# New orders for the tasks of all five engines in a four-layer graph network on one core

## The chip, the core and the metric

The kernel runs on one core of a Trainium2 chip. Five engines work side by side, each through its own list of instructions in order: TensorE (PE) multiplies, ScalarE (ACT) and VectorE (DVE) work elementwise, GpSimd (POOL) does a small power function here and issues three kinds of DMA, SyncE (SP) issues all others. They meet by semaphores alone. The metric is the device time of one launch in microseconds, the median of several runs.

## The reference

Sixteen graphs of 1024 nodes with 128 features pass through four layers that share one adjacency matrix; each layer's result is added to its input and normalised. Cut to what matters:

```python
x = _layernorm(x + relu(softmax(leaky_relu(s_i + t_j) + mask) @ H))           # layer 0, one head
x = _layernorm(x + elu(per head: softmax(leaky_relu(e_i + e_j) on edges) @ h)) # layer 1, 8 heads of 16
x = _layernorm(x + relu(layernorm((adj == 1) @ x / degree @ W + x @ self_w.T + b)))  # layer 2
x = _layernorm(x + per head: softmax(Wh @ Wh.T / sqrt(32) on edges) @ Wh)     # layer 3, 4 heads of 32
```

x is [16, 1024, 128] in float32, adj [16, 1024, 1024] in int32 with some 3% ones.

## The kernel before

Four batches are under way at once. Period f works on batch n = f + 1 in layer 0 and the preparation of layer 1, on batch f in the main part of layer 1, on batch k = f - 1 in layers 2 and 3, and on m = f - 2 in the end of layer 3. The periods run from f = -1 to 17; those of f = 2 to 14 all follow the same table, and f = 15 to 17 share one stretch.

**The work of a period.** Layer 1 has 32 pairs of units (`unit1`, 8 heads of 4): ACT, or for five pairs of a period DVE (`layer1_ramps`), makes a ramp of the source row of the head (`s1row`, three buffers); DVE masks it with the adjacency (L1672); PE multiplies it in (L1020, two units); DVE adds up each finished head (`head1`, L1680). `layer1_sum_all` (`sum1`, eight tiles, L1001) is a second sum on PE. For layer 2, PE does `layer2_self` and eight `layer2_sum` (L1067, L1070), ACT copies the self term to `yb`, and DVE takes both in `layer2_out` (from L1747), followed by statistics, affine part and `layer2_norm` (the DVE rows of L1483 that write `x` from `yb`). Its result is turned on PE (`layer3_turn`, L862 into `kp`), copied by ACT (`xbT`), projected (`layer3_project`, L1086 and L1092), copied twice by ACT (`w` and `shared`), and one half of the second copy is mirrored to the other partitions by two DMAs on SP (`spread_far`, L752), called the mirror copy below. The shift comes from the row maxima (`layer3_turn_maxima`, L1097). Then 16 times `layer3_scores` (L1122 where PE puts the mask in, and L1129), two exponentials on ACT (L1376), for eight of them a masking on DVE (L1818), and `layer3_values` on PE (L1146). `layer3_finish` on DVE (L1837) leads to the residual transfer on POOL (L822). Layer 0 has `layer0_turn` (L893), `layer0_project` (L905), its maximum and spread (L916, L920), eight units (L1272 on ACT, L1578 on DVE, L945 on PE), `layer0_finish` and `layer0_norm` (L1483 into `x`).

**The adjacency's way.** POOL copies a batch's matrix to a DRAM buffer as bf16 (`load_adjacency`, L829, "adjacency copy"), once the batch before has been turned out of that buffer. SP turns it by a DMA transpose (L734). POOL then narrows it to 8 bits in one of three buffers (`narrow_adjacency`, L818).

**What sets the order.** Each engine has tables that are written out by hand, one for each kind of period: a number for each task. `schedule` walks through the numbers and calls what has that number. The numbers of two engines have nothing to do with each other; only the order on each engine counts. What an engine waits for stands in the task's own code. The wait of `spread_sources` for a free buffer is by count: head h may be loaded when head h - 3 has all its edges.

Of the kernel before, what the change touches and what calls it, by code (L numbers as in the profile page):

```python
# [76 lines left out]
def graph_stack(nc, x, adj, L0_gnn_W, L0_gnn_a, L1_gnn_W, L1_gnn_a, L2_gnn_rel_weights, L2_gnn_self_w,  # L77
# [12 lines left out]
    B_RING, P_RING, P0_RING, R_RING, S_RING = 6, 4, 3, 6, 3  # L90
# [36 lines left out]
    with ExitStack() as ctx:  # L127
# [103 lines left out]
        rest2 = yf  # L231
# [260 lines left out]
        def schedule(tables, step):  # L492
# [3 lines left out]
            for stage, periods in zip(STAGE, SECTIONS):  # L496
                for s in range(STEPS):
# [23 lines left out]
            (dict(maxima1=93, maxima3=43, project0=[18, 20, 26], project1=89, project2=102, project3=40, scores3=[48,
                 52, 56, 60, 67, 69, 71, 73, 84, 85, 88, 90, 96, 98, 101, 103], self2=1, shift3=45, sources1=91,
                 spread0=46, spread1=95, sum1=[21, 22, 25, 29, 30, 31, 32, 33], sum2=[2, 3, 4, 5, 6, 11, 12, 13],
                 top0=36, turn0=[0, 17], turn1=87, turn2=99, turn3=37, turn_back=-1, unit0=[74, 75, 76, 77, 78, 79,
                 80, 81], unit1=[7, 8, 9, 10, 14, 15, 16, 19, 23, 24, 27, 28, 34, 35, 38, 39, 41, 42, 44, 47, 49, 50,
                 51, 53, 57, 58, 59, 61, 63, 64, 65, 66], values3=[54, 55, 62, 68, 70, 72, 82, 83, 86, 92, 94, 97,
                 100, 104, 105, 106]),),
            (dict(maxima1=92, maxima3=43, project0=[28, 29, 34], project1=90, project2=102, project3=41, scores3=[49,
                 53, 56, 58, 65, 70, 75, 82, 84, 86, 89, 93, 96, 100, 103, 105], self2=0, shift3=47, sources1=94,
                 spread0=48, spread1=97, sum1=[19, 24, 25, 26, 35, 36, 37, 38], sum2=[1, 2, 3, 6, 9, 12, 16, 17],  # L530
                 top0=44, turn0=[10, 20], turn1=88, turn2=98, turn3=39, turn_back=32, unit0=[72, 73, 74, 77, 78, 79,
                 80, 81], unit1=[4, 5, 7, 8, 11, 13, 14, 15, 18, 21, 22, 23, 27, 30, 31, 33, 40, 42, 45, 46, 50, 51,
                 52, 55, 59, 60, 61, 62, 66, 67, 68, 69], values3=[54, 57, 63, 64, 71, 76, 83, 85, 87, 91, 95, 99,
                 101, 104, 106, 107]),),
            (dict(maxima1=-1, maxima3=42, project0=[-1, -1, -1], project1=-1, project2=73, project3=39, scores3=[45,
                 47, 53, 58, 61, 63, 65, 66, 69, 72, 76, 79, 83, 90, 92, 93], self2=0, shift3=44, sources1=-1,
                 spread0=-1, spread1=-1, sum1=[16, 19, 24, 25, 28, 31, 32, 34], sum2=[1, 2, 3, 4, 8, 10, 13, 15],
                 top0=-1, turn0=[-1, -1], turn1=-1, turn2=71, turn3=35, turn_back=18, unit0=[-1, -1, -1, -1, -1, -1,
                 -1, -1], unit1=[5, 6, 7, 9, 11, 12, 14, 17, 20, 21, 22, 23, 26, 27, 29, 30, 33, 36, 37, 38, 40, 41,
                 43, 46, 48, 50, 51, 52, 55, 56, 57, 59], values3=[49, 54, 60, 62, 64, 67, 68, 70, 74, 75, 84, 89, 91,  # L540
                 94, 95, 97]), dict(maxima1=-1, maxima3=100, project0=[-1, -1, -1], project1=-1, project2=-1,
                 project3=98, scores3=[102, 103, 104, 107, 109, 111, 113, 115, 117, 119, 121, 123, 125, 127, 129,
                 131], self2=77, shift3=101, sources1=-1, spread0=-1, spread1=-1, sum1=[-1, -1, -1, -1, -1, -1, -1,
                 -1], sum2=[78, 80, 81, 82, 85, 86, 87, 88], top0=-1, turn0=[-1, -1], turn1=-1, turn2=-1, turn3=96,
                 turn_back=99, unit0=[-1, -1, -1, -1, -1, -1, -1, -1], unit1=[-1, -1, -1, -1, -1, -1, -1, -1, -1, -1,
                 -1, -1, -1, -1, -1, -1, -1, -1, -1, -1, -1, -1, -1, -1, -1, -1, -1, -1, -1, -1, -1, -1],
                 values3=[105, 106, 108, 110, 112, 114, 116, 118, 120, 122, 124, 126, 128, 130, 132, 133]),
# [21 lines left out]
            (dict(cut1=[84, 87], cut1_second=[93, 94], elu=57, exp3=[32, 33, 36, 37, 40, 41, 45, 46, 49, 50, 53, 54,
                 55, 56, 59, 61, 65, 66, 68, 69, 71, 72, 74, 75, 77, 78, 81, 82, 85, 86, 90, 91], exps0=31, exps1=79,  # L570
                 first2=88, out3=[52, 67, 80, 96], prepare0=43, project0=[10, 13, 16], project1=73, project3=25,
                 ramps=[2, 3, -1, 4, 5, 6, -1, 7, 9, 11, 12, 14, 15, 18, 20, 21, 24, 26, 28, -1, 29, 30, -1, 34, 35,
                 -1, 38, 39, 42, 44], ramps_ahead=[89, 95], second2=92, self2=1, sources1=76, sum1=[17, 19, 22],
                 turn0=[0, 8], turn1=70, turn2=83, turn3=23, unit0=[47, 48, 51, 58, 60, 62, 63, 64], wide3=27),),
            (dict(cut1=[83, 85], cut1_second=[89, 90], elu=66, exp3=[31, 32, 34, 35, 38, 39, 41, 42, 46, 47, 53, 54,
                 58, 59, 62, 63, 64, 65, 68, 69, 71, 72, 74, 76, 77, 78, 82, 84, 87, 88, 91, 92], exps0=37, exps1=79,
                 first2=86, out3=[49, 67, 81, 95], prepare0=48, project0=[15, 17, 25], project1=73, project3=26,
                 ramps=[0, 1, -1, 2, 3, 4, -1, 5, 6, 9, 10, 11, 13, 14, 16, 18, 19, 22, 28, -1, 29, 30, -1, 33, 36,
                 -1, 40, 43, 44, 45], ramps_ahead=[94, 96], second2=93, self2=8, sources1=75, sum1=[20, 21, 23],
                 turn0=[7, 12], turn1=70, turn2=80, turn3=24, unit0=[50, 51, 52, 55, 56, 57, 60, 61], wide3=27),),  # L580
# [108 lines left out]
        def _(sp):  # L689
# [1273 lines left out]
```

How the kernel before makes its waits and increments, by code:

```python
            def load(dst, src, done):  # L690
                sp.dma_start(dst, src).then_inc(done, 16)
# [4 lines left out]
            def load_x(b):  # L696
                if x1_ready.any_before(b):
                    sp.wait_ge(x1_ready.sem, x1_ready.before(b))
                sp.dma_start(x0[:], rows(x, b)).then_inc(x_loaded.sem, 16)
# [1 line left out]
            def spread_sources(b, h):  # L701
                if h >= S_RING:
                    sp.wait_ge(edges_ready.sem, edges_ready.of(b, (h - S_RING + 1) * T // 2))
                elif edges_ready.any_before(b):
                    sp.wait_ge(edges_ready.sem, edges_ready.before(b))
                sp.dma_start(s1row[:, h % S_RING, :], s1_dram[h:h + 1].broadcast_to([P, N])) \
                    .then_inc(s1_loaded[h].sem, 16)
# [1 line left out]
            def store_row(b):  # L710
                sp.wait_ge(row0_ready.sem, row0_ready.of(b))
                if s0_loaded.any_before(b):
                    sp.wait_ge(s0_loaded.sem, s0_loaded.before(b))
                sp.dma_start(s0_dram.rearrange("a (t p) -> (a t) p", p=P), row0[:]).then_inc(s0_stored.sem, 16)
# [1 line left out]
            def spread_row(b):  # L717
                sp.wait_ge(s0_stored.sem, s0_stored.of(b))
                sp.dma_start(c0[:], s0_dram.broadcast_to([P, N])).then_inc(s0_loaded.sem, 16)
# [1 line left out]
            def store_sources(b):  # L721
                sp.wait_ge(s1_copied.sem, s1_copied.of(b))
                if edges_ready.any_before(b):
                    for h in range(H1):
                        sp.wait_ge(s1_loaded[h].sem, s1_loaded[h].before(b))
```

## Time and profile before

| | us |
|---|---|
| median of 3 runs | 2438.4 |
| lowest, highest | 2432.07, 2440.47 |
| the profiled execution | 2435.11 |
| its span, first to last instruction | 2433.3 |

The profiled execution spends 1.8 us outside the span. Times of rows are counted from the span's start. A row of a timeline gives start, length, engine, line, operation, what it writes and reads, how often, and in square brackets how long its engine stood still before it and what it waited for. The mean granted clock of PE was 0.978 of full speed; it was below full in the first 180 us, in the last 100, and in three short dips between.

### The profile page before, as it was taken

What the parts mean: (1) busy time and instruction counts of PE and PEld (TensorE: products, weight loads), DVE (VectorE), ACT (ScalarE), POOL (GpSimd) and SP (SyncE); (2) the same over time, 40 slices, a digit from 0 to 9 for tenths busy, and PEclk for the clock granted to TensorE, in tenths of its full rate; (3) what the DMA queues carried; (4) which work ended last, traced back from release to release, by engine and by line L of the source; (5) the groups of instructions that cost most, each with busy time, mean ns of one, the idle gap of its engine ahead of it and who ended that gap; (6) DMA issues with size and microseconds to landing.
All of it is one profiled execution on the core that took longest, in us unless ns stands there. A gap on an engine that the chain in (4) does not pass through costs nothing.

```text
span 2433.3 us, 56856 instructions
## 1 busy us (share of the span) xinstructions
PE 2226.6 (92%) x23701; PEld 1498.8 (62%) x23701; DVE 1986.4 (82%) x4206; ACT 1946.5 (80%) x2166; POOL 180.4 (7%) x134
## 2 busy tenths in 40 slices
PE   6668999999999999999999999999999999998876
PEld 5667576575856657585665757566585765658431
DVE  4677788889888888988889888888988878897666
ACT  3958698887889878788987879898787988878734
POOL 0000000010000001000000100001010000100010
PEclk8879999999999999999999999999999999999989
DMA  4552061523315253341524324143432415301000
GB/s 92 140 114 71 5 145 53 121 75 92 82 47 132 59 113 80 76 92 45 131 71 105 88 54 114 44 123 79 105 89 45 114 53 123 80 27 48 24 18 18
DMA packets 190865, 193.77 MB, mean 80 GB/s; under 512 B 129368, under 2 KB 165328, under 8 KB 187728
## 3 DMA queue, kind: packets, MB, share of 16 engines
q1 hardware_dynamic: 183008, 132.99, 20.0%
q0 software_dynamic: 7600, 57.15, 12.0%
q8 instruction: 187, 3.06, 0.5%
q14 instruction: 70, 0.57, 0.1%
HBM read 151.26 MB, written 40.43 MB: 79 GB/s over the span
## 4 chain that ended last, share of the span: by engine, by line
PE 68%; ACT 11%; issue 6%; DVE 6%; DMA 2%; POOL 0%; SPq 0%; POOLq 0%; ACTq 0%; DVEq 0%
PE kp L1146 12%; PE fp L1020 10%; PE kp L1129 9%; PE fp L945 8%; PE kp L1001 7%; ACT weight L1376 5%; PE kp L1122 4%; PE kp L1070 4%; DMA shared<-shared 2%; PE kp L1067 2%; ACT ramp L1328 1%; PE fp L1038 1%; PE fp L869 1%; PE kp L1086 1%; PE kp L1163 1%
## 5 line engine op out<-in xcount | busy, mean ns | idle before, releaser
L1328 ACT ACTIVATE ramp<-s1row,tbig 128x1024 fp8e4<-128x1024 f32 x854 | 909.3, 1148 | 11.9 <-DVE weight L1672 11.9
L1376 ACT ACTIVATE weight<-kp,shift 128x1024 f32<-128x1024 f32 x480 | 511.2, 1111 | 206.4 <-PE kp L1129 188.3
L1146 PE MATMUL kp<-weight,w 128*33 128x512 f32 x1920 | 456.8, 599 | 17.9 <-DVE weight L1818 6.6
L1672 DVE TENSOR_TENSOR weight<-ramp,AT 128x512 int32<-128x512 int32 x512 | 343.3, 689 | 153.7 <-PE fp L1020 98.7
L1020 PEld LDWEIGHTS fp<-vh_parts,weight 128*128 128x128 fp8e4 x8192 | 389.9, 97 | 83.7 <-DVE weight L1672 41.2
L1020 PE MATMUL fp<-vh_parts,weight 128*128 128x102 bf16 x8192 | 417.6, 208 | 21.0 <-DVE weight L1672 15.5
L1818 DVE SCALAR_TENSOR_TENSOR weight<-AT,weight 128x1024 f32<-128x1024 fp8e4 x272 | 321.5, 1219 | 37.6 <-ACT weight L1376 37.3
L1129 PE MATMUL kp<-shared 32*128 32x512 f32 x1920 | 274.7, 641 | 13.8 <-ACT weight L1376 13.7
L1146 PEld LDWEIGHTS kp<-weight,w 128*33 128x33 f32 x1920 | 94.4, 110 | 312.7 <-issue 224.0
L945 PEld LDWEIGHTS fp<-features,weight 128*128 128x128 f32 x1840 | 207.9, 192 | 28.7 <-issue 27.0
L945 PE MATMUL fp<-features,weight 128*128 128x129 f32 x1840 | 213.4, 276 | 5.0 <-DVE weight L1578 4.9
L1001 PE MATMUL kp<-vh_parts,AT 128*128 128x136 bf16 x3072 | 212.5, 229 | 0.3 <-ACT vh_rest L1233 0.3
L1001 PEld LDWEIGHTS kp<-vh_parts,AT 128*128 128x128 fp8e4 x3072 | 205.0, 97 | 0.9 <-ACT vh_rest L1233 0.5
L1272 ACT ACTIVATE weight<-xfT,v0neg,v0s 128x1024 f32<-128x1024 f32 x123 | 149.4, 1244 | 37.2 <-PE fp L945 36.2
L1070 PE MATMUL kp<-elu,AT 128*128 128x128 bf16 x1920 | 171.8, 221 | 0.0
L1067 PE MATMUL kp<-y_hi,AT 128*128 128x129 bf16 x960 | 167.7, 222 | 2.7 <-DVE elu L1732 2.7
L1578 DVE SCALAR_TENSOR_TENSOR weight<-weight,v,AT 128x1024 f32<-128x1024 f32 x123 | 153.1, 1281 | 15.5 <-ACT weight L1272 14.8
L1680 DVE TENSOR_REDUCE vh<-fp 128x272 f32<-128x816 f32 x128 | 128.4, 1003 | 42.2 <-PE fp L1020 41.9
L1122 PE MATMUL kp<-AT,big 128*128 128x512 fp8e4 x480 | 127.6, 382 | 28.7 <-DMA shared<-shared 21.8
L1129 PEld LDWEIGHTS kp<-shared 32*128 32x128 f32 x1920 | 76.1, 183 | 125.7 <-issue 67.9
L1070 PEld LDWEIGHTS kp<-elu,AT 128*128 128x128 fp8e4 x1920 | 149.7, 98 | 0.2
L795 POOL TENSOR_TENSOR bsmall<-bsmall,half_neg 128x8 f32<-128x8 f32 x32 | 60.7, 1897 | 917.4 <-DVE bsmall L1478 917.4
(251 smaller groups left out, 2715.9 us busy)
## 6 DMA issues: line engine op xcount, KB each, us to landing
s1row<-s_rows_dram SPq DMA_DIRECT2D x128, 512.0 KB, 4.1
adj_bf_dram<-in_adj_dram POOLq DMA_DIRECT2D x15, 2048.0 KB, 13.3
AT<-turned POOLq DMA_DIRECT2D x15, 1024.0 KB, 7.5
x<-in_x_dram SPq DMA_DIRECT2D x16, 512.0 KB, 4.4
out_dram<-elu SPq DMA_DIRECT2D x16, 512.0 KB, 3.2
xfT<-s_row_dram SPq DMA_DIRECT2D x15, 512.0 KB, 4.6
shared<-shared SPq DMA_DIRECT2D x30, 256.0 KB, 3.5
elu<-x POOLq DMA_DIRECT2D x15, 512.0 KB, 4.7
```

Of the source, the lines that this page charges most:

```text
L945: last = pe.matmul(sums0(b)[:, g, n * (D + 1):(n + 1) * (D + 1)], ring0(b, jt)[:, t * P:(t + 1) * P], h0[:, jt, :], start=(jt == 0 and n = ...
L1001: last = pe.matmul(kp[:, SUM_A_BANKS[t // PER], n * H1 * C1:(n + 1) * H1 * C1].rearrange("p (h c) -> p h c", h=H1), AT[:, third, jt, t * P ...
L1020: last = pe.matmul(fp[:, 1 + t // 4, col:col + 2 * PARTS * C1], edges[:, u % B_RING, t * P:(t + 1) * P], vh_parts[:, jt, h, :, :, :].rearr ...
L1067: pe.matmul(sums2(b)[:, g, col:col + D + 1], lhsT, y2_hi[:, jt, :], start=(jt == 0), stop=False, skip_group_check=True)
L1070: last = pe.matmul(sums2(b)[:, g, col:col + D], lhsT, low2(b)[:, jt, k, :], start=False, stop=(jt == T - 1 and k == 1), skip_group_check=True)
L1122: pe.matmul(score_banks(b, w)[:, x, :], big[:], AT[:, third, 2 * J + x, n * HALF:(n + 1) * HALF], start=True, stop=False, skip_group_check ...
L1129: last = pe.matmul(score_banks(b, w)[:, x, :], mine[:, jt * P:(jt + 1) * P], mine[:, n * HALF:(n + 1) * HALF], start=v in masks(b), stop=True,
L1146: last = pe.matmul(kp[side(h), 0, :], values3(b)[:, (2 * J + x) * H3 + h, :], weight3[:, w % P_RING, x * HALF:(x + 1) * HALF], start=(J == ...
L1328: act.activation(ramp[:, u % R_RING, :], s1row[:, h % S_RING, :] if b or h else kp_pair, ACT.Relu, bias=tbig1[:, jt, h:h + 1], scale=BIG, ...
L1376: act.activation(weight3[:, w % P_RING, :], score_banks(b, w).rearrange("p a n -> p (a n)"), ACT.Exp, bias=shifts3(b)[:, h:h + 1], scale=R ...
L1672: dve.tensor_tensor(edge_words[:, u % B_RING:u % B_RING + 2, :], ramp_words[:, u % R_RING:u % R_RING + 2, :], AT_words[:, third, jt:jt + 2 ...
L1818: dve.scalar_tensor_tensor(out=mine, in0=AT[:, third, 2 * J:2 * J + 2, n * HALF:(n + 1) * HALF], scalar=0.0, in1=mine, op0=ALU.is_equal if ...
```

## The change

All numbers of the tables for PE, ACT, DVE, POOL and SP are new; no task is added or taken away. One wait is added, on SP, which concerns batch 0 alone. The diff of the tables is long and tells little, so one row of POOL's and SP's each stands for it:

```diff
@@ ON_POOL, periods f = 2 to 14
-            (dict(adjacency=6, narrow=1, residual3=3, rstd0=5, rstd1=7, rstd2=0, rstd3=2, rstd_tail=4),),
+            (dict(adjacency=3, narrow=4, residual3=2, rstd0=6, rstd1=7, rstd2=0, rstd3=1, rstd_tail=5),),
@@ ON_SP, periods f = 2 to 14
-            (dict(adjacency=0, far=5, out=10, sources=[2, 3, 4, 7, 9], sources_ahead=[12, 13, 14], spread_row=8,
-                 store_row=6, store_sources=11, x=1),),
+            (dict(adjacency=0, far=7, out=10, sources=[3, 2, 5, 4, 6], sources_ahead=[13, 14, 12], spread_row=9,
+                 store_row=8, store_sources=11, x=1),),
@@ spread_sources
                     sp.wait_ge(edges_ready.sem, edges_ready.before(b))
+                if b == 0 and h == S_RING:
+                    sp.wait_ge(s1_loaded[0].sem, s1_loaded[0].of(0))
                 sp.dma_start(s1row[:, h % S_RING, :], s1_dram[h:h + 1].broadcast_to([P, N])) \
```

The numbers of `sources` are those of heads 3, 4, 5, 6 and 7. So SP now issues head 4's row before head 3's, head 6's before head 5's, and head 7's before the mirror copy. Line numbers behind L706 are higher by 2 in the changed kernel.

POOL in one steady period, before: from the first of two layer-2 statistics (`bsmall`) to batch n's last statistic (`fsmall` is layer 1's).

```order
L795 TENSOR_TENSOR bsmall<-bsmall,half_neg 128x8
L818 DMA AT<-turned 128x8192
L795 TENSOR_TENSOR bsmall<-bsmall,half_neg 128x8
L822 DMA elu<-x 128x1024
L795 TENSOR_TENSOR tsmall<-tsmall,half_neg 128x8
L795 TENSOR_TENSOR small<-small,half_neg 128x8
L829 DMA adj_bf_dram<-in_adj_dram 64x16384
L795 TENSOR_TENSOR fsmall<-fsmall,half_neg 128x8
```

The same period of POOL, after:

```order
L797 TENSOR_TENSOR bsmall<-bsmall,half_neg 128x8 x2
L824 DMA elu<-x 128x1024
L831 DMA adj_bf_dram<-in_adj_dram 64x16384
L820 DMA AT<-turned 128x8192
L797 TENSOR_TENSOR tsmall<-tsmall,half_neg 128x8
L797 TENSOR_TENSOR small<-small,half_neg 128x8
L797 TENSOR_TENSOR fsmall<-fsmall,half_neg 128x8
```

The adjacency copy moved from behind layer 0's statistic (`small`) to right behind the residual transfer (`elu<-x`), and the narrowing transfer (`AT<-turned`) from ahead of that transfer to behind it.

PE in a steady period, before, from the last `layer1_sum_all` to the first scores:

```order
L1001 MATMUL kp<-vh_parts,AT 128x136 x96
L862 MATMUL kp<-ident,x 128x128 x8
L1020 MATMUL fp<-vh_parts,weight 128x102 x16
L1086 MATMUL kp<-rhs,xbT 128x128 x8
L1092 MATMUL kp<-xbT,rhs 128x512 x2
L1020 MATMUL fp<-vh_parts,weight 128x102 x16
L1097 MATMUL kp<-ident,qmax 4x128
L916 MATMUL fp<-ident,st 33x128
L1020 MATMUL fp<-vh_parts,weight 128x102 x32
L1101 MATMUL kp<-qdiag,ones 128x4
L920 MATMUL fp<-tmost,ones 128x1
L1122 MATMUL kp<-AT,big 128x512 x4
```

The same stretch of PE, after:

```order
L864 MATMUL kp<-ident,x 128x128 x8
L1022 MATMUL fp<-vh_parts,weight 128x102 x16
L907 MATMUL fp<-rhs,xfT 128x130 x2
L1088 MATMUL kp<-rhs,xbT 128x128 x8
L1094 MATMUL kp<-xbT,rhs 128x512 x2
L1022 MATMUL fp<-vh_parts,weight 128x102 x16
L1099 MATMUL kp<-ident,qmax 4x128
L1022 MATMUL fp<-vh_parts,weight 128x102 x16
L1103 MATMUL kp<-qdiag,ones 128x4
L1022 MATMUL fp<-vh_parts,weight 128x102 x16
L1124 MATMUL kp<-AT,big 128x512 x4
```

Layer 0's third projection (L907) came in ahead of `layer3_project`, and the maximum of layer 0 and its spread (L916 and L920 before) went behind the first scores. On ACT the copy of the self term now stands ahead of layer 0's first copy; in the period of f = 0, DVE does `layer0_finish` before the last four pairs of units and not behind them.

## Rows read from the trace of the kernel before

**Rows 1.** The page's first part: busy time, share of the span, instructions.

```profile
PE 2226.6 (92%) x23701; PEld 1498.8 (62%) x23701; DVE 1986.4 (82%) x4206; ACT 1946.5 (80%) x2166; POOL 180.4 (7%) x134
```

**Rows 2.** Windows view, one steady period: stretch, length, busy time by engine, PE clock, DMA.

```profile
1382.53:1525.84 143.31, 136.86 (x1479) 92.21 (x1479) 122.21 (x261) 121.27 (x136) 11.11 (x8) 1.00 0.36 86
```

**Rows 3.** Waits of PE in that period: total us, times, longest.

```profile
PE kp L1097 <- DVE qmax L1796: 1.4, 1, 1.4
PE kp L1122 <- DMA shared<-shared: 1.3, 1, 1.3
PE kp L1129 <- ACT weight L1376: 1.0, 2, 0.5
PE fp L1020 <- DVE weight L1672: 0.7, 1, 0.7
PE fp L905 <- ACT features L1233: 0.6, 1, 0.6
PE kp L1086 <- ACT xbT L1233: 0.4, 1, 0.4
```

**Rows 4.** Timeline of PE, from the end of layer 2's sums to the first scores.

```profile
1493.87 0.88 PE L1020 MATMUL fp<-vh_parts,weight 128*128 128x102 bf16 x16
...
1512.03 0.68 PE L905 MATMUL fp<-rhs,xfT 128*128 128x130 f32 x4
...
1518.83 1.04 PE L862 MATMUL kp<-ident,x 128*128 128x128 f32 x8
...
1520.98 2.05 PE L1086 MATMUL kp<-rhs,xbT 128*128 128x128 f32 x16 [0.40 <-ACT xbT L1233]
...
1530.35 1.02 PE L1122 MATMUL kp<-AT,big 128*128 128x512 fp8e4 x4 [1.31 <-DMA shared<-shared]
```

**Rows 5.** Timeline of DVE: the start of `layer2_out` and `layer2_norm`.

```profile
1494.30 0.29 DVE L1747 TENSOR_SCALAR deg<-kp 128x3 f32<-128x3 f32 x3 [0.70 <-ACT yb L1233]
...
1515.33 2.14 DVE L1483 TENSOR_SCALAR x<-yb,bsmall 128x128 f32<-128x128 f32 x8
```

**Rows 6.** Timeline of POOL: its three DMA issues of a period.

```profile
1442.32 0.58 POOL L829 DMA_DIRECT2D adj_bf_dram<-in_adj_dram  x1
...
1503.03 0.59 POOL L818 DMA_DIRECT2D AT<-turned  x1
...
1515.72 0.96 POOL L822 DMA_DIRECT2D elu<-x  x1 [0.46 <-DVE elu L1837]
```

**Rows 7.** The mirror copy: its issue on SP, and all its landings.

```profile
1525.84 1.11 SPq L752 DMA_DIRECT2D shared<-shared  x2
...
DMA to landing us min/median/max: 2.9/3.5/3.9
```

**Rows 8.** DMA view of 1442.32 to 1456, the adjacency copy: packets, MB, share; landing.

```profile
DMA packets 89, 2.15 MB, mean 157 GB/s; under 512 B 16, under 2 KB 16, under 8 KB 23
...
q0 software_dynamic: 80, 2.10, 75.8%
...
adj_bf_dram<-in_adj_dram POOLq DMA_DIRECT2D x1, 2048.0 KB, 13.6
```

**Rows 9.** DMA view of 83.92 to 85.30: a source row issued behind the narrowing transfer.

```profile
q0 software_dynamic: 33, 0.27, 98.1%
...
s1row<-s_rows_dram SPq DMA_DIRECT2D x1, 512.0 KB, 5.5
```

**Rows 10.** DMA view of 1498.91 to 1500.29: a source row alone.

```profile
q1 hardware_dynamic: 12, 0.05, 17.6%
...
s1row<-s_rows_dram SPq DMA_DIRECT2D x1, 512.0 KB, 3.7
```

**Rows 11.** Timelines of ACT and DVE at the end of the period f = 0.

```profile
149.52 1.02 ACT L1233 ACTIVATE xfT<-fp 128x1024 f32<-128x1024 f32 x1 [12.26 <-PE fp L862]
...
138.05 0.13 DVE L1589 RECIPROCAL rec<-kp 128x3 f32<-128x3 f32 x1
...
145.33 2.14 DVE L1483 TENSOR_SCALAR x<-x,small 128x128 f32<-128x128 f32 x8 [0.87 <-POOL small L795]
```

More of the change, by code:

```diff
@@ L521, in graph_stack @@
[L521 to L527, printed above, removed]
@@ L569, in graph_stack @@
[L569 to L574, printed above, removed]
@@ L575, in graph_stack @@
[L575 to L580, printed above, removed]
@@ new lines, in graph_stack @@
+            (dict(cut1=[82, 85], cut1_second=[93, 95], elu=62, exp3=[33, 34, 36, 37, 39, 40, 43, 44, 46, 47, 52, 55,
+                 59, 61, 63, 64, 65, 66, 68, 69, 71, 72, 74, 75, 78, 79, 83, 84, 87, 88, 90, 91], exps0=41, exps1=76,
+                 first2=86, out3=[54, 67, 80, 96], prepare0=48, project0=[9, 16, 27], project1=73, project3=28,
+                 ramps=[0, 1, -1, 2, 3, 6, -1, 8, 10, 11, 13, 14, 15, 17, 18, 21, 22, 23, 24, -1, 26, 30, -1, 31, 32,
+                 -1, 35, 38, 42, 45], ramps_ahead=[89, 94], second2=92, self2=4, sources1=77, sum1=[12, 19, 20],
+                 turn0=[5, 7], turn1=70, turn2=81, turn3=25, unit0=[49, 50, 51, 53, 56, 57, 58, 60], wide3=29),),
@@ new lines, in graph_stack @@
+            (dict(cut1=[83, 86], cut1_second=[89, 90], elu=64, exp3=[32, 33, 35, 36, 40, 41, 43, 44, 46, 47, 53, 54,
+                 58, 59, 62, 63, 65, 66, 68, 69, 71, 72, 74, 75, 77, 78, 82, 84, 87, 88, 91, 92], exps0=39, exps1=80,
+                 first2=85, out3=[49, 67, 81, 96], prepare0=48, project0=[18, 23, 29], project1=73, project3=26,
+                 ramps=[0, 1, -1, 2, 3, 4, -1, 5, 6, 8, 9, 10, 11, 12, 15, 16, 19, 21, 25, -1, 28, 30, -1, 31, 34, -1,
+                 37, 38, 42, 45], ramps_ahead=[94, 95], second2=93, self2=7, sources1=76, sum1=[13, 20, 22],
+                 turn0=[14, 17], turn1=70, turn2=79, turn3=24, unit0=[50, 51, 52, 55, 56, 57, 60, 61], wide3=27),),
@@ L659, in graph_stack @@
         ON_POOL = [
[L660 to L666 removed]
+            (dict(adjacency=0, narrow=-1, residual3=-1, rstd0=1, rstd1=-1, rstd2=-1, rstd3=-1, rstd_tail=-1),),
@@ L667, in graph_stack @@
         ]
         ON_SP = [
-            (dict(adjacency=-1, far=-1, out=-1, sources=[-1, -1, -1, -1, -1], sources_ahead=[1, 2, 3], spread_row=-1,
+            (dict(adjacency=-1, far=-1, out=-1, sources=[-1, -1, -1, -1, -1], sources_ahead=[3, 1, 2], spread_row=-1,
                  store_row=-1, store_sources=0, x=-1),),
-            (dict(adjacency=1, far=-1, out=-1, sources=[2, 3, 4, 5, 8], sources_ahead=[10, 11, 12], spread_row=7,
-                 store_row=6, store_sources=9, x=0),),
-            (dict(adjacency=0, far=7, out=-1, sources=[1, 2, 3, 8, 9], sources_ahead=[11, 12, 13], spread_row=6,
-                 store_row=5, store_sources=10, x=0),),
@@ L675, in graph_stack @@
-            (dict(adjacency=0, far=5, out=10, sources=[2, 3, 4, 7, 9], sources_ahead=[12, 13, 14], spread_row=8,
-                 store_row=6, store_sources=11, x=1),),
-            (dict(adjacency=-1, far=4, out=6, sources=[0, 1, 2, 3, 5], sources_ahead=[-1, -1, -1], spread_row=-1,
+            (dict(adjacency=1, far=-1, out=-1, sources=[3, 2, 4, 8, 7], sources_ahead=[10, 12, 11], spread_row=6,
+                 store_row=5, store_sources=9, x=0),),
+            (dict(adjacency=1, far=7, out=-1, sources=[2, 4, 3, 6, 5], sources_ahead=[13, 12, 11], spread_row=9,
+                 store_row=8, store_sources=10, x=0),),
@@ L678, in graph_stack @@
+            (dict(adjacency=0, far=7, out=10, sources=[3, 2, 5, 4, 6], sources_ahead=[13, 14, 12], spread_row=9,
+                 store_row=8, store_sources=11, x=1),),
+            (dict(adjacency=-1, far=4, out=6, sources=[1, 0, 3, 2, 5], sources_ahead=[-1, -1, -1], spread_row=-1,
                  store_row=-1, store_sources=-1, x=-1), dict(adjacency=-1, far=7, out=8, sources=[-1, -1, -1, -1, -1],
```

180 lines of the change are left out of this document (93 added, 87 removed).

## The prediction

> **What bounds the kernel now.** I read the busy shares first: TensorE (PE) is busy 92% of the span, no other engine more than 82% [rows 1]. So only what lets PE stand still can be won or lost by an order. Then I cut out one period of the steady part, from one issue of the mirror copy to the next: 143.31 us with PE busy 136.86, so 6.45 us idle, at full granted clock [rows 2]. Thirteen periods (f = 2 to 14) run by this table and repeat it. The waits of PE in that period [rows 3] name the losses: 1.4 for the row maxima of layer 3, 1.3 for the mirror copy (the DMA inside `shared`), 1.0 for exponentials, 0.7 for edge weights, 0.6 and 0.4 for two ScalarE (ACT) copies. The profiled execution took 2435.1 us (span 2433.3); the median of the runs is 2438.4, so 3.3 is added at the end.
>
> **Part 1, the new order on PE, VectorE (DVE) and ACT in the 13 steady periods.** Nothing is added or removed, so durations stay and I follow starts. All times here are in the period shown.
> Three waits of PE stand between the end of layer 2's sums (1493.87) and `layer3_project` (1520.98): 0.74 before a unit of edges, 0.65 between two `layer0_project`, 0.40 before `layer3_project` [rows 3, 4]. In the new order two `layer1_sum_all` stand ahead of the first, three between the second pair, and a `layer0_project` covers the copy before the third: 1.8 us of waits lose their cause. What is late next is DVE. `layer2_out` starts at 1494.30, held by ACT's copy of the self term, and DVE then works without a pause to 1517.37 = 1515.33 + 2.04 (the eight tiles of `layer2_norm`, until the next start): 23.07 us [rows 5]. PE begins `layer3_turn` at 1518.83 [rows 4], 1.46 behind it. ACT's copy moves ahead of a copy of about 0.5, so DVE starts some 0.45 earlier and ends at 1516.9. PE: 24.96 us from 1493.87 to 1518.83, less 0.74 and 0.65, less 0.5 (the third `layer0_project`, a row at 1512.03 [rows 4], goes behind) plus 0.4 (a `layer0_turn` that comes in), is 23.5; begun at 1493.4, as that turn left the part before, it arrives at 1516.9 too. So `layer3_turn` starts near 1517.0, with the copies of ACT queued behind each other `layer3_project` near 1519.4, 1.6 earlier than 1520.98. From there to the first scores 9.4 us pass (1520.98 to 1530.35 [rows 4]), through two copies, the mirror copy and its landing; PE only waits in them, so the two tiny tasks that the new order takes out of this stretch (`layer0` maximum and its spread, 0.2) save nothing here.
> Behind the first scores PE had no wait for 29 us. There ACT gets the exponents of layer 0 between two pairs of exponentials, and three edge ramps stand before others; following PE, ACT and DVE task by task I find one new wait of 0.2. Later the scores of pair 11 move ahead of `layer1_turn_maxima` and `layer1_sources`, which takes away the 0.44 in the 1.0 of exponentials. Sum: 1.6 - 0.2 + 0.4 = 1.8; since I neglect semaphore latencies I take 1.6 per period, from 0.3 (DVE or ACT late at `layer3_turn`) to 1.9. 13 x 1.6 = 20.8 us gained.
>
> **Part 2, the new order of the DMA issues.** This is where I expect the loss. POOL issued the adjacency copy (2 MB) at 1442.32, when no other transfer was under way, and the narrowing transfer at 1503.03, both far from the mirror copy at 1525.84 [rows 6, 7]. Now both stand behind the residual transfer, which waits for `layer3_finish` and goes at 1515.72 [rows 6]; with DVE 0.5 earlier and `layer3_finish` ahead of one unit that is near 1514.8, and the adjacency copy follows at once, near 1515.8. It needs 13.6 us to land; its 64 large packets (80 less 16 under 512 B) kept 16 engines busy for 75.8% of 13.68 us, so 4 packets of 2.6 us on each engine [rows 8]. Behind the residual's own 3 us they would fill 1519 to 1529. On SP the last source row (head 7) now stands ahead of the mirror copy; it is issued near 1521.3 and its 8 packets per engine come first. The mirror copy is issued near 1524.2, in the middle of all that, and must land before PE may go on: its 2.9 to 3.9 us [rows 7] have no slack, as PE already waits 1.3 for it.
> What such a meeting costs: a source row issued at 83.92, while the narrowing transfer was under way, got no packet in its first 1.38 us (all 33 were the other's, 98.1% of the engines) and landed after 5.5 us [rows 9]; an undisturbed one had 12 packets in the same 1.38 us and landed after 3.7 [rows 10]. That is +1.8 us against packets of 0.66 us (98.1% of 16 x 1.38 us over 33), though the overlap was short. The engines thus do not share finely; a transfer waits for its turn. Bounds for the mirror copy: 1.2 (bandwidth shared in halves during its 1.2 us of data) and, for turns of one large packet ahead of each of its two halves, 2 x 2.6 = 5.2 in the slowest engine. I take 3.0, between one turn (half a packet, 1.3, plus the source row's 0.7) and two (3.9). 12 periods load a further adjacency (f = 2 to 13): 12 x 3.0 = 36 us lost; from 14 to 62.
> The Trainium skill (DMA: Bandwidth & Descriptors, Queues, rings and completion order) says that an engine changes between rings only at packet boundaries, and that a semaphore's write waits for every earlier write of that engine, whatever its queue. By that rule alone both turns are paid, 5.2 us, and the sum below would be 26 us higher. The trace agrees with the turns [rows 9], the second half of the rule no row shows.
>
> **Part 3, the first batches.** ACT waits 12.26 us at the end of the period f = 0 for batch 1's layer 0: DVE does `layer0_finish` from 138.05 to 143.46 (145.33 less a wait of 0.87 for POOL and the 1.00 of a head) and only then `layer0_norm` [rows 11]. It now stands ahead of the last four units, in time in which ACT was the slow one: 5.4 + 0.9 = 6.3 gained. Against it the adjacency copy of batch 2 moves from behind this point to right behind the narrowing transfer that [rows 9] shows under way, where the source rows of heads 4 and 3 are loaded; by [rows 9] 1.8 for one, and I take 2.3. Net -4, from -8 to +2. **The added wait**: SP waits, once, for head 0's row of batch 0, ahead of head 3's; that row is issued with the first three, and head 3's can go only when head 1's edges are made, which the whole of ACT's ramps for two heads precede. Behind it queue head 3's row and batch 1's layer 0 row. Nobody waits: 0. The tables of the last periods differ in single neighbours: 0, within 2.
>
> **Sum.** 2435.1 - 20.8 + 36 - 4 = 2446.3, plus 3.3: **2450 us**, 0.5% slower. Its own range, with 2.0 to 4.5 for the mirror copy: 2438 to 2468.
>
> **The rivals.**
> A, not slower: the mirror copy gets through (the engines' turns are short or the adjacency copy begins later than I place it), while part 1 holds. 2435.1 - 20.8 - 4 + 3.3 = 2414. For it: the slack elsewhere is real, and [rows 9] shows small packets against small ones only. Against it: no slack at the mirror copy. It decides from 1.6 us downwards: below that the periods get shorter. 20%.
> B, about equal: delay 1.2 to 2.0, 2428 to 2438, most of it within 0.3%. 20%.
> C, much slower: an engine finishes all it has of POOL's transfers before the mirror copy: 1529 plus up to 5.4 us of narrowing (8 packets of 0.66) against 1525.3, so 4 to 9 us; with 8, 2435.1 - 24.8 + 96 + 3.3 = 2510. [Rows 9] is what such a run-out looks like. 10%.
> D, part 1 fails: `layer3_norm`'s input comes late and a wait at `layer3_turn` replaces the three removed; gain 0.3 a period, delay 3.0: 2435.1 - 4 - 4 + 36 + 3.3 = 2466. 10%.
> Forecast: 40%.
>
> **How the numbers follow.** A measurement of this kernel tells 0.3%, 7.3 us, from no change. Faster by more (below 2431): A and a third of B, 27%. Within: the rest of B and the low end of the forecast, 18%. Slower: 55%. The range 2412 to 2472 leaves out C and little else.
>
> **What would show it.** Right: PE's wait for the mirror copy grows from 1.3 to 3 or more per period, the landing of that DMA from 3.5 to 6 or so, in 12 periods, the residual at once followed by the adjacency copy; PE's waits for `features`, `xbT` and edge weights gone; ACT's 12.3 halved. The steady period would be 144.7. Wrong: a period of 141.7 with the mirror copy at 3.5 (A), or a wait of PE at `layer3_turn` over 0.5 (D). If the adjacency copy were issued before 1510 in this frame, part 2 falls altogether.

## The result and the profile after

| | before | after |
|---|---|---|
| median, us | 2437.3 (4 runs) | 2570.3 (4 runs) |
| lowest, highest | 2432.07, 2440.47 | 2569.34, 2571.48 |
| the profiled execution's span | 2433.3 | 2567.6 |

The ratio is 1.055, interval 1.053 to 1.056: 5.5% slower. I had forecast 2450 and a range up to 2472; the direction was right and the size was not, nor did the range hold it.

The page of the changed kernel, its first part (busy time and share), against [rows 1]; TensorE does the same 23701 instructions, is busy 34.5 us longer and yet has a smaller share of the span.

```profile
PE 2261.1 (88%) x23701; PEld 1521.8 (59%) x23701; DVE 1985.5 (77%) x4206; ACT 1943.1 (76%) x2166; POOL 186.4 (7%) x134
```

One steady period, from one mirror copy to the next, as in [rows 2] (stretch, length, busy time of PE, of its weight loads, DVE, ACT and POOL, granted clock, DMA share, GB/s), and PE's waits in it, against [rows 3].

```profile
1459.89:1614.95 155.06, 139.57 (x1479) 93.57 (x1479) 122.07 (x261) 121.10 (x136) 11.54 (x8) 0.96 0.33 77
```

```profile
PE kp L1124 <- DMA shared<-shared: 12.2, 1, 12.2
PE kp L1099 <- DVE qmax L1798: 1.4, 1, 1.4
PE kp L864 <- DVE x L1485: 0.5, 1, 0.5
PE kp L1131 <- ACT weight L1378: 0.5, 1, 0.5
```

The period is 11.75 us longer than the 143.31 of [rows 2]. PE stands still for 155.06 - 139.57 = 15.49 us against 6.45. Of this the wait for the mirror copy went from 1.31 to 12.20 (+10.89), and all other waits together from 5.14 to 3.29 (-1.85). The remaining 2.71 is busy time: the same 1479 matmuls took 139.57 and not 136.86, at a granted clock of 0.96 and not 1.00.

Over the whole launch, by the issues of the mirror copy (line 752 before, 754 after; starts and length on SP): the first rows of after are

```profile
233.42 1.17 SPq L754 DMA_DIRECT2D shared<-shared  x2
372.33 1.11 SPq L754 DMA_DIRECT2D shared<-shared  x2
...
2236.42 1.89 SPq L754 DMA_DIRECT2D shared<-shared  x2
```

and the second and the fourteenth issue of before were at 377.47 and 2100.65. So after is 5.1 us ahead at the second mirror copy; then come twelve periods of 155.34 on average (1864.09 / 12) against 143.60 (1723.18 / 12), 140.9 lost; behind them the rest of the launch is 1.5 shorter (331.2 against 332.7). -5.1 + 140.9 - 1.5 = 134.3, the difference of the spans. It is all in the twelve periods in which POOL issues a further adjacency copy.

The timeline of POOL in the changed kernel, the place of [rows 6]: all three transfers now go within 2 us, 10 us ahead of the mirror copy at 1459.89.

```profile
1449.67 0.93 POOL L824 DMA_DIRECT2D elu<-x  x1 [0.49 <-DVE elu L1839]
1450.30 0.85 POOL L831 DMA_DIRECT2D adj_bf_dram<-in_adj_dram  x1
1450.84 0.87 POOL L820 DMA_DIRECT2D AT<-turned  x1
```

Landings of the mirror copy in the changed kernel, against 2.9/3.5/3.9 in [rows 7], and PE at the first scores, against [rows 4]:

```profile
DMA to landing us min/median/max: 3.1/14.7/16.1
```

```profile
1475.40 1.86 PE L1124 MATMUL kp<-AT,big 128*128 128x512 fp8e4 x4 [12.20 <-DMA shared<-shared]
```

Two DMA views of the changed kernel say what the engines did meanwhile. From the issue of head 7's source row (1456.64, just ahead of the mirror copy on SP) not one packet of SP's queue q1 was served for 3.5 us; all belonged to POOL's queue q0, in packets of 32 KB:

```profile
q0 software_dynamic: 30, 0.98, 130.5%
```

Then, from 1462.9 to 1470, the two queues were served strictly in turn, one packet of the one and one of the other:

```profile
q0 software_dynamic: 113, 0.84, 58.8%
q1 hardware_dynamic: 114, 0.45, 17.6%
```

An engine gave 0.59 us on average to each packet of POOL's and 0.17 to each of SP's (58.8% and 17.6% of 16 x 7.1 us, over the counts). That is the suspicion the experiments test: **each packet of the mirror copy pays one whole packet of POOL's, and so does each packet of the source row that stands ahead of it in the same queue, as long as POOL's queue has any.** A row of 512 KB is 8 packets of 4 KB for each engine, a half of the mirror copy 4; the under-512-byte packets in these views are extra ones, which I take for the semaphores' writes and count as one turn for each transfer: 9 + 5 + 5 = 19 turns.

POOL's queue had fewer left. Of the adjacency copy it was the last of four packets on each engine, of the narrowing transfer (128 packets of 8 KB) eight. From 1460.15 to 1465 the engines served 18 packets of q0 and 18 of q1, from 1465 to 1471 135 and 136; then q0 ran out. This is the view of the rest, 1471 to 1475.4, in which 0.48 MB of the mirror copy's 0.52 are served:

```profile
q1 hardware_dynamic: 150, 0.48, 40.3%
q0 software_dynamic: 25, 0.07, 8.2%
```

So the source row ahead of it paid nearly all of the turns, and the mirror copy came behind the row and behind nearly everything that POOL had issued. 19 turns of 0.59 + 0.17 us would be 14.4, from 1460.15 to 1474.6, and PE's wait ended at 1475.40; that this comes near is luck, as only some nine turns were that dear, the one beside a 32 KB packet much dearer, and the last ten cheaper.

### The profile page after: what moved, and what is told of

The parts are those of the page before. It is cut to its first block, busy times and chain, and to the rows that moved or that the text cites. A ratio compares the mean times of both kernels' runs of the same rounds, so it can differ in the third digit from the quotient of the medians.

```text
span 2567.6 us, 56857 instructions
## 1 busy us (share of the span) xinstructions
PE 2261.1 (88%) x23701; PEld 1521.8 (59%) x23701; DVE 1985.5 (77%) x4206; ACT 1943.1 (76%) x2166; POOL 186.4 (7%) x134
## 4 chain that ended last, share of the span: by engine, by line
PE 58%; ACT 15%; DMA 9%; DVE 9%; issue 8%; SPq 0%; POOL 0%; ACTq 0%; POOLq 0%; DVEq 0%
PE kp L1148 14%; PE kp L1131 11%; ACT ramp L1330 10%; PE fp L947 8%; DMA shared<-shared 8%; PE fp L1022 7%; PE kp L1124 5%; ACT weight L1378 2%; PE kp L1003 2%; PE fp L871 2%; PE kp L1072 1%; PE fp L864 1%; PE fp L1040 1%; PE kp L1088 1%; DVE weight L1674 1%
## 5 line engine op out<-in xcount | busy, mean ns | idle before, releaser
L1022 PE MATMUL fp<-vh_parts,weight 128*128 128x102 bf16 x8192 | 434.8, 211 | 20.5 <-DVE weight L1674 15.1
L1022 PEld LDWEIGHTS fp<-vh_parts,weight 128*128 128x128 fp8e4 x8192 | 401.8, 99 | 80.3 <-DVE weight L1674 41.5
L1131 PE MATMUL kp<-shared 32*128 32x512 f32 x1920 | 284.4, 663 | 10.3 <-ACT weight L1378 10.1
L1124 PE MATMUL kp<-AT,big 128*128 128x512 fp8e4 x480 | 138.8, 406 | 156.8 <-DMA shared<-shared 153.8
L947 PEld LDWEIGHTS fp<-features,weight 128*128 128x128 f32 x1840 | 210.8, 193 | 34.3 <-issue 32.7
L947 PE MATMUL fp<-features,weight 128*128 128x129 f32 x1840 | 219.0, 279 | 0.7 <-DVE weight L1580 0.7
L1124 PEld LDWEIGHTS kp<-AT,big 128*128 128x128 bf16 x480 | 37.8, 100 | 227.4 <-issue 163.0
## 6 DMA issues: line engine op xcount, KB each, us to landing
shared<-shared SPq DMA_DIRECT2D x30, 256.0 KB, 14.7
```

What stands on the lines that cost most here:

```text
L947: last = pe.matmul(sums0(b)[:, g, n * (D + 1):(n + 1) * (D + 1)], ring0(b, jt)[:, t * P:(t + 1) * P], h0[:, jt, :], start=(jt == 0 and n = ...
L1022: last = pe.matmul(fp[:, 1 + t // 4, col:col + 2 * PARTS * C1], edges[:, u % B_RING, t * P:(t + 1) * P], vh_parts[:, jt, h, :, :, :].rearr ...
L1124: pe.matmul(score_banks(b, w)[:, x, :], big[:], AT[:, third, 2 * J + x, n * HALF:(n + 1) * HALF], start=True, stop=False, skip_group_check ...
L1131: last = pe.matmul(score_banks(b, w)[:, x, :], mine[:, jt * P:(jt + 1) * P], mine[:, n * HALF:(n + 1) * HALF], start=v in masks(b), stop=True,
```

## Experiments

Theory 1 is that the meeting of POOL's transfers with the mirror copy makes the whole loss. In its form 1a the engines change the queue after every packet; in form 1b they finish POOL's packets first. The two differ in time only where POOL's queue still has packets when the mirror copy is through; in the changed kernel, by the view above, it has none. Theory 2 is that the new orders of PE, ACT and DVE carry a good part.

| kernel | median us | ratio to before, interval | PE's wait for the mirror copy, us in all |
|---|---|---|---|
| e1: POOL's old table in the changed kernel | 2411.1 | 0.989, 0.988 to 0.991 | 12.4 |
| e2: POOL's new table in the kernel before | 2579.8 | 1.058, 1.056 to 1.060 | 135.0 |
| e3: changed, mirror copy ahead of head 7's row | 2550.7 | 1.046, 1.045 to 1.048 | 138.7 |
| e4: changed, narrowing back | 2506.8 | 1.029, 1.027 to 1.030 | 100.1 |
| e5: changed, adjacency copy back | 2445.9 | 1.003, 1.002 to 1.005 | 34.3 |
| e6: changed, adjacency copy in 8 KB packets | 2566.0 | 1.053, 1.050 to 1.055 | 151.4 |
| e7: the same in 2 KB packets | 2489.1 | 1.022, 1.020 to 1.023 | 72.3 |
| e8: before, mirror copy delayed | 2553.9 | 1.048, 1.047 to 1.050 | 95.1 |
| e9: e1 again | 2408.8 | 0.989, 0.988 to 0.990 | 13.7 |
| e10: e9, mirror copy ahead of head 7's row | 2413.4 | 0.991, 0.990 to 0.993 | 16.0 |

The kernel before waits 21.8 us for it in all, the changed one 153.8.

**e1, POOL's order back.**

```diff
-            (dict(adjacency=3, narrow=4, residual3=2, rstd0=6, rstd1=7, rstd2=0, rstd3=1, rstd_tail=5),),
+            (dict(adjacency=6, narrow=1, residual3=3, rstd0=5, rstd1=7, rstd2=0, rstd3=2, rstd_tail=4),),
```

and so for the tables of POOL in the other stages.

> The changed kernel with the old table of POOL alone; PE, ACT, DVE and SP keep the new one. Theory 1 (the loss is the meeting of POOL's two transfers with the mirror copy): the mirror copy lands again after 3.5 to 4 us, PE waits 1 to 2 us for it, the period is 141.5 to 142, the granted clock is back at 0.975 or more, and the time is some 2412 us, ratio 0.99 to before. Theory 2 (a good part of the loss comes from the new orders of PE, ACT and DVE, and the mirror copy only shows it): over 2445 us. If the source row that now stands ahead of the mirror copy matters by itself: 2 us more a period, 2436.

2411.1 us: theory 2 falls, and with it the idea that a source row ahead of the mirror copy costs anything while POOL is quiet. The whole table of POOL is worth 159 us, and what is left of the change is a gain of 1.1%. One of its periods at full clock, and one that is not:

```profile
1370.37:1511.87 141.50, 137.05 (x1479) 92.58 (x1479) 122.09 (x261) 120.98 (x136) 11.55 (x8) 1.00 0.36 87
...
1084.00:1227.89 143.89, 139.80 (x1479) 93.75 (x1479) 122.07 (x261) 121.20 (x136) 11.55 (x8) 0.98 0.36 85
```

141.50 is what the prediction gave for part 1 alone (141.7). But only two of twelve periods are so; they take 142.7 on average.

**e2, POOL's order alone.** The same table, the other way round: the new one in the kernel before, where the mirror copy stands ahead of head 7's row.

> The kernel before with the new table of POOL alone; on SP the mirror copy stands ahead of head 7's source row. Theory 1a (an engine changes between the queues after every packet, so that each of the mirror copy's 8 packets of an engine waits for one of POOL's): the landing takes 9 to 11 us, PE's wait grows by 6 to 7, with 1 more for the clock 12 x 7.8 = 94 us, 2530. Theory 1b (the engines finish all of POOL's packets first): landing 14 to 15 us as in the changed kernel, 2570 to 2590. My prediction's single turns: landing 6 to 7, 2475.

2579.8: of the numbers given beforehand, this fits that of 1b and not that of 1a. A period of e2 and PE's largest wait in it:

```profile
1472.06:1628.26 156.20, 140.19 (x1479) 94.01 (x1479) 122.55 (x261) 121.30 (x136) 10.63 (x8) 0.96 0.34 79
```

```profile
PE kp L1122 <- DMA shared<-shared: 10.9, 1, 10.9
```

The DMA views show the order. From the mirror copy's issue to 1476.9 only POOL's queue was served, with 32 KB packets (first fence); from 1477 to 1482 both queues, packet for packet (second), so POOL's packets had not gone first.

```profile
q0 software_dynamic: 17, 0.56, 78.6%
...
shared<-shared SPq DMA_DIRECT2D x2, 256.0 KB, 11.6
```

```profile
q0 software_dynamic: 111, 0.78, 74.5%
q1 hardware_dynamic: 114, 0.40, 21.2%
```

What my number for 1a lacked is first the entry, as I call the time from a transfer's issue to its first packet: 4.9 us, in which 17 large packets began, one on each engine behind the one under way. And it lacked the narrowing: ten turns (2 x 5) beside its eight packets on each engine, at 0.76 us, are 1477 + 7.6 = 1484.6; PE went on at 1486.14. With ten turns against eight packets both forms end at nearly the same time, so the total of e2 can't tell them apart.

**e3, mirror copy first.**

```diff
-            (dict(adjacency=0, far=7, out=10, sources=[3, 2, 5, 4, 6], sources_ahead=[13, 14, 12], spread_row=9,
+            (dict(adjacency=0, far=6, out=10, sources=[3, 2, 5, 4, 7], sources_ahead=[13, 14, 12], spread_row=9,
```

> The changed kernel with head 7's source row behind the mirror copy in the steady periods. Theory 1a (a turn for every packet, and the source row's 8 packets an engine stand in the same queue ahead of the mirror copy): landing 10 to 11 us and not 14.7, some 5 us less a period with the clock, 2510. Theory 1b (all of POOL's packets first): no change, 2570.

2550.7, 20 us less and not 60: a third of what 1a gave, and more than the nothing of 1b. In the DMA view of its mirror copy at 1451.66 the entry is long again. Up to 1457.4, 5.7 us, three packets of q1 in all were served (first fence); then 1:1 (second, 1457.5 to 1464).

```profile
q0 software_dynamic: 32, 1.05, 98.2%
q1 hardware_dynamic: 3, 0.01, 0.6%
```

```profile
q0 software_dynamic: 136, 1.01, 76.0%
q1 hardware_dynamic: 133, 0.48, 24.9%
```

In the changed kernel the source row, issued 3.3 us ahead, had made that entry for the mirror copy. With the row behind it, the mirror copy pays the entry itself, and its own ten turns still take it through nearly all of the narrowing's eight packets. The two halves land 12.7 us after the issue on average, against 14.3 in the changed kernel's period; 1.6 us a period is the 20 us.

**e4 and e5, one transfer at a time.** Of POOL's table in the steady periods, e4:

```diff
-            (dict(adjacency=3, narrow=4, residual3=2, rstd0=6, rstd1=7, rstd2=0, rstd3=1, rstd_tail=5),),
+            (dict(adjacency=4, narrow=1, residual3=3, rstd0=6, rstd1=7, rstd2=0, rstd3=2, rstd_tail=5),),
```

> The changed kernel with the narrowing transfer back between the two statistics of layer 2; the adjacency copy stays right behind the residual transfer. Theory 1a: the adjacency copy's last packets end some 12 us after the residual's issue, then the source row and the mirror copy run freely; landing 6.5 to 8 us, PE waits 4 to 5, 8 to 9 us less a period than in the changed kernel, 2465 to 2475. Were the adjacency copy alone the cause: 2560. Were the narrowing alone the cause: 2415.

and e5:

```diff
-            (dict(adjacency=3, narrow=4, residual3=2, rstd0=6, rstd1=7, rstd2=0, rstd3=1, rstd_tail=5),),
+            (dict(adjacency=6, narrow=3, residual3=2, rstd0=5, rstd1=7, rstd2=0, rstd3=1, rstd_tail=4),),
```

> The changed kernel with the adjacency copy back behind layer 0's statistic, some 70 us away from the mirror copy, and the narrowing transfer left behind the residual transfer. Theory 1a (a turn for every packet): the narrowing's 8 packets of 0.62 us an engine end before the mirror copy's first packet comes, the landing is 3.5 to 4.5 us, the time 2411 to 2422. Theory 1b (POOL's packets first) says the same here; if the narrowing alone were a cause as large as the 64 us by which e4 and the changed kernel differ: 2475.

2506.8 and 2445.9. Against e1, the adjacency copy alone costs 96 us, the narrowing alone 35, both 159. Both numbers were expected smaller (2470; 2411 to 2422), so neither transfer is harmless there, and both together cost 28 us more than the sum of the two. (e1 has POOL's old tables in the other stages as well, which e4 and e5 have not; there they are worth 4 us, 1.7 up to the second mirror copy and 2.4 from the fourteenth on.) In e4 the turns are to be seen at their dearest: from 1423 to 1427, with the source row and the mirror copy waiting, POOL's 32 KB packets and SP's 4 KB packets were served one for one,

```profile
q0 software_dynamic: 24, 0.79, 94.4%
q1 hardware_dynamic: 24, 0.10, 6.5%
```

2.5 us for each of POOL's (94.4% of 64 us over 24). In these 4 us the queue of small packets got 6.5% of the engines. In e5 the landing's median is 4.5 us where e1 has 3.5, and PE waits 34.3 in all, 22 more; of the other 13 of the 35 us, 10 are busy time of PE (2260.3 against 2249.9 us for the same matmuls).

**e6 and e7, the size of the packets.** The same bytes, in an order that cannot be joined to longer packets (g = 16, c = 4 for 8 KB; g = 64, c = 1 for 2 KB); this is e6:

```diff
-                pool.dma_start(adj_dram, adj[bass.ds(b, 1)].rearrange("b i j -> (b i) j")) \
+                pool.dma_start(adj_dram.rearrange("(a g c) j -> g a (c j)", g=16, c=4),
+                               adj[bass.ds(b, 1)].rearrange("b (a g c) j -> g (b a) (c j)", g=16, c=4)) \
```

> The changed kernel; the adjacency copy walks through the same 2 MB in an order that makes packets of 8 KB, not 32 KB. Theory 1a (a turn for every packet): the source row gets its first turn some 2 us earlier and the mirror copy follows earlier: landing 11 to 12 us, 3 to 4 us less a period with the clock, 2520 to 2530. Theory 1b (POOL's packets first, so that only the bytes count): no change, 2570.

> As e6, in packets of 2 KB. Theory 1a: a turn of the adjacency copy costs 0.16 us, the 16 packets of source row and mirror copy an engine pass at 0.33 us each, the mirror copy lands after some 5 us, PE waits 2.4 and the time is near 2426 to 2440, though nothing is moved away. Theory 1b: 2570.

2566.0 and 2489.1. With 2 KB the loss falls by 81 us though POOL and SP issue in the changed kernel's order and the same bytes are carried; under 1b next to nothing could have moved. 8 KB changed next to nothing, where I had expected 45 us. The views of e6 (1452.49 to 1455.8, then 1456 to 1468) show why:

```profile
q0 software_dynamic: 87, 0.71, 103.0%
```

```profile
q0 software_dynamic: 251, 1.93, 81.6%
q1 hardware_dynamic: 253, 0.91, 22.0%
```

The first 3.3 us again belong to POOL's queue alone, with packets of 8 KB as with packets of 32 KB: the entry does not shrink with the packet. And 251 to 253 is one for one at 0.62 and 0.17 us, 0.79 us a turn, which for 19 turns is 15.0 us, from 1455.9 to 1470.9; e6's mirror copy, issued at 1455.27, had its halves landed 13.2 us later on average, and PE's wait of 11.6 ended at 1470.81. POOL's queue had some 16 packets left on each engine, about as many as SP had turns: as in the changed kernel, the mirror copy got through only when nearly all of POOL's bytes had gone, and these bytes are the same in packets of 8 KB. That is why the time stayed. With 2 KB the packets of q0 cost 0.19 us each (62.6% of 16 x 8 us over 419, from 1409 to 1417), behind an entry of 3.3 us that is wholly POOL's (340 packets):

```profile
q0 software_dynamic: 340, 0.70, 111.3%
```

```profile
q0 software_dynamic: 419, 0.86, 62.6%
q1 hardware_dynamic: 294, 1.03, 40.9%
```

SP's cost 0.18 (40.9% over 294). 19 turns of 0.37 us are 7.0; the median landing is 7.6 us, against 14.7. My 5 us for it had left out the entry. Here SP's turns ran out first. When PE went on, at 1418.10, POOL's queue still had nearly the whole narrowing transfer (1.05 MB) to serve, as the view from there to 1424 shows; this is what tells 1a from 1b.

```profile
q0 software_dynamic: 154, 0.99, 80.9%
```

**e8, the price of standing still.** In the kernel before, ahead of each mirror copy:

```diff
                 sp.wait_ge(wT_ready.sem, wT_ready.of(b))
+                for i in range(4):
+                    sp.dma_start(pause_row[0:1, :], L2_gnn_ln_beta.rearrange("(a d) -> a d", a=1)).then_inc(paused.sem, 16)
+                    sp.wait_ge(paused.sem, paused.of(b, 16 * (i + 1)))
                 for side in range(2):
```

> The kernel before; ahead of each mirror copy SP makes four DMAs of 512 bytes, one after the other, and waits for each: PE stands some 8 us longer, with next to no traffic beside it. Theory K (standing still lowers the clock granted afterwards): PE's busy time in a period grows from 136.9 to 139 or more though it does the same work, and the period grows by 2 to 3 us more than the wait. If it was the DMA traffic that slowed PE in the changed kernel: busy time stays 136.9, the period grows by the wait alone. Time by K: 15 x 10.5 = 158 over before, 2595; without: 2555.

2553.9. The total equals the number given for the other theory, but by accident: the four small DMAs took 4.8 us, not 8 (their first was issued at 1445.06, the mirror copy at 1449.87). A period of e8, and PE's wait in it:

```profile
1449.87:1600.31 150.44, 139.15 (x1479) 93.03 (x1479) 122.62 (x262) 121.36 (x136) 10.67 (x8) 0.98 0.35 82
```

```profile
PE kp L1127 <- DMA shared<-shared: 6.1, 1, 6.1
```

7.13 us longer than [rows 2]: 4.84 of standing still and 2.29 of busy time, for the same work, at a clock of 0.98, with the same DMA traffic but for a few bytes. Theory K stands: the busy time that the changed kernel loses is the clock's, and not the traffic's.

**e9 and e10, the version that beats both.** e9 is e1's kernel; e10 has e3's edit in it as well.

> The kernel of e1 once more, beside the next one on the same chip: 2411 us, 1.1% under before, if e1 stands.

> e1's kernel with head 7's source row behind the mirror copy in the steady periods, as before. By the turns, the source row's packets are through when the mirror copy's come, since none of POOL's stand between: nothing gained, 2409 to 2413. If the row ahead in the queue delays the mirror copy by itself: PE's wait for it falls by 0.3 to 0.5 us a period, with the clock 2405 or less.

e1's gain repeats: 2408.8, 1.1% under the kernel before. e10 at 2413.4 (2405.0 to 2418.1) can't be told from it: head 7's row ahead of the mirror copy is harmless with POOL quiet.

## Why the prediction was wrong in size

**Part 1, the orders of PE, DVE and ACT: the waits right, the total in part luck.** 1.6 to 1.8 us a period were forecast. In the changed kernel the waits other than for the mirror copy fell by 1.85. The three waits named are gone; in their place stands 0.52 at `layer3_turn` for DVE's `layer2_norm`, close to the forecast that PE and DVE arrive there together. It is just over the 0.5 that was named as rival D's sign, but D's gain of only 0.3 a period is out: without POOL's part (e1) a period at full clock is 141.50, forecast 141.7. The launch of e1 took 2411, forecast 2414 as rival A, and there luck helped. Its twelve periods gave 10.4 us (1723.18 against 1712.82) where 12 x 1.6 = 19 were forecast, since ten of them were not at full clock. The first batches (6.8) and the end of the launch (3.8) made up for it.

**Part 2, the DMA issues: the place right, the size wrong by 3.6.** Everything was late where the text put it: the transfers' order, no slack at the mirror copy, the source row's packets first. Forecast were 3.0 us a period from bounds of 1.2 and 5.2; measured 10.89. The step that failed is "turns of one large packet ahead of each of its two halves": it let the mirror copy pay once for each half. An engine changes the queue behind each packet (114 to 113 in the view above), so every packet in SP's queue pays, and those ahead of the mirror copy pay first. In its place the runs showed a mirror copy that came behind nearly all that POOL had issued, with PE's wait 10.89 us longer. Three terms were left out:
- the source row's packets, for which I took their own duration (0.7), pay turns too: the row stood against the last 32 KB packet and nearly the whole narrowing, to 1471;
- the narrowing transfer, behind the adjacency copy, is part of what has to go first (from 1465 to 1471, 0.62 us a packet); I had let it count in rival C alone;
- the entry: 3.3 to 3.5 us pass before a source row's first packet, and up to 5.7 before the mirror copy's (e3). What makes it was not tested.

The row on which I rested, [rows 9], was read amiss, and so was the agreement with turns for which the prediction cites it. 33 packets to none in 1.38 us looked like a transfer that holds the engines for a turn. But an undisturbed transfer has no packet either in its first 0.89 us (1498.91 to 1499.80, the one of [rows 10]), so this was mostly the entry, and hardly a turn is in it. Its +1.8 us was a price with little of the other queue left behind it, not one for a meeting of full length. Rival C had the nearest number (8 us, 2510) and 10% of the chance. Its mechanism, that the engines finish POOL's packets first, is not what e7 and the views of e2 and e3 show. Its outcome, that the mirror copy waits for all of POOL's transfers with the narrowing among them, is what the changed kernel did.

**The clock: left out.** The sum counted waits and took durations as fixed. A longer wait of PE is followed by matmuls at the lower clock. Windows of the changed kernel around the wait that ended at 1475.40 (the clock is the third number from the end):

```profile
1459.89:1463.20 3.31, 2.19 (x35) 1.86 (x35) 2.81 (x9) 3.31 (x6) 0.00 (x0) 1.00 1.18 210
1463.20:1469.00 5.80, 0.00 (x1) 0.00 (x0) 2.94 (x4) 3.21 (x4) 0.00 (x0) 0.84 0.67 167
1469.00:1475.40 6.40, 0.00 (x0) 0.03 (x1) 0.00 (x0) 0.00 (x0) 0.00 (x0) 0.50 0.67 165
1475.40:1480.00 4.60, 4.60 (x20) 1.64 (x21) 0.29 (x2) 0.62 (x1) 0.00 (x0) 0.50 0.01 4
1480.00:1485.00 5.00, 5.00 (x72) 3.60 (x70) 3.46 (x6) 3.69 (x4) 0.00 (x0) 0.92 0.34 106
```

While PE stood, the clock went from 2.4 to 1.2 GHz (1.00 to 0.50), and it stayed there through the first 4.6 us of full work. It costs 2.7 us in this period; over the twelve periods PE is busy 1674.5 us and was 1645.4 before, 29 us of the 134.

**Part 3, the first batches: the number right by luck.** Forecast -4; after is 5.1 ahead at the second mirror copy. ACT's wait of 12.26 became 4.94:

```profile
157.06 1.02 ACT L1235 ACTIVATE xfT<-fp 128x1024 f32<-128x1024 f32 x1 [4.94 <-PE fp L864]
```

But the row starts 7.5 us later than the 149.52 of [rows 11], and at the first mirror copy after is 7.2 behind (233.42 against 226.16). The term that was too small is the adjacency copy brought forward, taken at 2.3: e1, which leaves it late, has its first mirror copy at 225.20, 8.2 earlier than after. What it held up was not the source rows of heads 4 and 3 alone but also layer 0's row, which goes through DRAM behind them in SP's queue. Both kernels issue its store at 96.86; SP issued the reload at 100.64 in e1 and at 111.81 in after, and DVE waited:

```profile
DVE xfT L1562 <- DMA xfT<-s_row_dram: 7.8, 1, 7.8
```

The way from 7.2 behind to 5.1 ahead lies between the first two mirror copies (138.91 us, before 151.31) and was not taken apart. The added wait of SP was put at nothing; e1 holds it as well and is 6.8 ahead at the second mirror copy, so no loss of its shows. The tables of the last periods: -1.5, forecast 0 within 2.

Put together, with the one period shown for all twelve: 12 x (10.89 - 1.85 + 2.71) = 141.0, less 5.1 and 1.5, is 134.4, of which the forecast had 36 - 20.8 - 4 = 11.

## What to carry to other kernels

A small transfer on which the busiest engine waits must be priced, when it meets bulk transfers of another queue, by **turns**. Take the entry (here 3.3 to 5.7 us). Then count on each engine its packets and all packets ahead of it in its own queue, and beside it what the bulk queue still has. Each turn costs one packet of both queues, until one queue is empty; where the bulk queue is empty first, as here, the small transfer has waited for all of it. So keep bulk issues away from such a place by their own length. Where they can't be moved, cut them so small that the turns run out before the bulk does: 2 KB for 32 KB gave back 81 of the 134 us here, 8 KB next to nothing. Add to a new wait of TensorE the clock that it costs afterwards. And before the gain of a new order on the compute engines is believed, list the DMA issues that it moves and set them beside the transfers that have no slack.

## What the runs showed of the hardware that I had not expected

- While both queues had packets, they were served about one for one whatever their sizes: 114 to 113, 253 to 251 and, with 32 KB against 4 KB, 24 to 24. With 2 KB packets (e7) it was 116 to 110 from 1409 to 1412, but 419 to 294 over the whole stretch to 1417, which I can't explain. The Trainium skill (DMA: Bandwidth & Descriptors, Queues, rings and completion order) says that an engine goes round its queues packet by packet; the trace agrees, for what it records as a packet.
- A source row got its first packet 3.3 to 3.5 us after its issue when the other queue had a backlog, with packets of 2, 8 or 32 KB alike; the mirror copy, where it went first beside 32 KB packets, took 4.9 (e2) and some 5.7 us (e3). In the kernel before, alone, the mirror copy had its first six packets within 1.16 us of its issue at 1525.84.
- Fewer waits can cost clock. In e1's period that starts at 1084.00 the clock falls right behind the mirror copy's wait, though that wait was only 0.8 us; the kernel before, which stands still more (6.5 us a period against 4.1 to 4.5), keeps full clock in ten of its twelve periods. Windows of e1:

```profile
1084.00:1087.80 3.80, 2.57 (x35) 2.16 (x35) 2.89 (x10) 3.80 (x6) 0.00 (x0) 0.86 0.56 141
1087.80:1093.20 5.40, 4.70 (x21) 1.79 (x22) 3.25 (x6) 3.55 (x4) 0.00 (x0) 0.50 0.00 2
1093.20:1100.00 6.80, 6.80 (x105) 4.89 (x102) 5.31 (x9) 5.52 (x6) 0.00 (x0) 0.97 0.25 80
```

  Over the twelve periods e1 is busy 1664.7 us and before 1645.4, 1.6 us more a period, against 2.5 us less of waiting. That its remaining waits now lie closer together may be the reason; no run tests it.
